# A gated transformer block in fp32 parts: the feed-forward stage rebuilt as one chunk pipeline, with its first weights split during the projection

## The reference

```python
xn = layernorm(x)                                   # x: (4, 1024, 256) float32
qkv = xn @ w_qkv                                    # 16 heads of 16
s = softmax(causal(q k^T / 4)) v @ w_out
f = xn
for i in range(6):                                  # feed-forward chain
    h = gelu(f @ W1[i].T + B1[i])                   # 256 -> 1024
    f = h @ W2[i].T + B2[i] + f                     # 1024 -> 256
    if i < 5: f = layernorm(f) * LN_G[i] + LN_B[i]
out = x + s * silu(f)
```

## Time and profile before

| | us |
|---|---|
| three executions | 1802.08, 1802.11, 1807.77 |
| median | 1802.11 |
| span of the profiled execution | 1806.1 |
| TensorE matmul busy | 1716.2 (95%) |
| VectorE busy | 1149.1 (64%) |
| ScalarE busy | 958.0 (53%) |
| GpSimd busy | 323.2 (18%) |

### The profile page before, as it was taken

The page is one execution under the profiler, slowest core; times in us unless marked ns, Lnnn a source line. Parts: engine busy times, 40 slices in busy tenths (PEclk is TensorE's granted clock), DMA queues, the critical chain, the costliest instruction groups (busy, mean ns, idle before and its releaser), DMA issues. The chain is left out here.

```text
span 1806.1 us, 33624 instructions
## 1 busy us (share of the span) xinstructions
PE 1716.2 (95%) x11664; PEld 1312.9 (73%) x11664; DVE 1149.1 (64%) x2325; ACT 958.0 (53%) x1364; POOL 323.2 (18%) x317
## 2 busy tenths in 40 slices
PE   6979999999999999999999999997999989999947
PEld 5869999999999989999999998875444433444236
DVE  7846666666666656666666643366877866877326
ACT  5834555555555545555555554432666665666723
POOL 3511111111111111111111111110121211121214
PEclk9989999999999999999999999998999998999969
DMA  6940000000000000000000050003474754574113
GB/s 206 306 140 13 12 17 16 13 12 17 13 9 12 17 16 12 13 17 12 16 12 12 0 83 24 23 24 64 76 112 75 109 84 73 88 107 73 48 57 137
DMA packets 104427, 97.97 MB, mean 54 GB/s; under 512 B 26636, under 2 KB 88588, under 8 KB 104316
## 3 DMA queue, kind: packets, MB, share of 16 engines
q1 hardware_dynamic: 104256, 96.39, 23.9%
q10 hardware_dynamic: 60, 0.10, 0.0%
HBM read 62.15 MB, written 29.62 MB: 51 GB/s over the span
## 5 line engine op out<-in xcount | busy, mean ns | idle before, releaser
L626 ACT ACTIVATE m_hid<-m_h_ps,m_b1s 128x512 f32<-128x512 f32 x384 | 264.3, 688 | 571.0 <-PE m_h_ps L752 558.9
L687 DVE TENSOR_TENSOR m_hidl<-m_hid,m_hidh 128x512 fp32r<-128x512 f32 x384 | 307.4, 809 | 323.9 <-ACT m_hidh L628 322.8
L129 DVE TENSOR_REDUCE mx<-a_s_ps 128x1 f32<-128x512 f32 (+3 forms) x570 | 341.2, 656 | 91.3 <-PE a_s_ps L117 87.8
L1003 ACT ACTIVATE a_prob<-a_st_ps 128x1024 f32<-128x1024 f32 (+1 forms) x320 | 289.9, 938 | 168.5 <-PE a_st_ps L1153 123.0
L752 PE MATMUL m_h_ps<-xth,shared 128*128 (+1 forms) x768 | 269.8, 397 | 12.3 <-DVE shared L655 12.2
L763 PE MATMUL m_y_ps<-shared,m_hidh 128*128 128x256 f32 x1536 | 277.9, 281 | 0.0
L628 ACT ACTIVATE m_hidh<-m_h_ps,m_b1s 128x512 fp32r<-128x512 f32 x384 | 261.8, 682 | 0.0
L763 PEld LDWEIGHTS m_y_ps<-shared,m_hidh 128*128 128x128 f32 x1536 | 246.6, 189 | 12.0 <-DVE m_hidl L687 0.4
L602 POOL TENSOR_TENSOR y<-y,m_b2s 128x1024 f32<-128x1024 f32 x47 | 112.8, 2400 | 708.3 <-DVE y L663 708.3
L763 PE MATMUL m_y_ps<-m_w2h,m_hidh 128*128 128x256 f32 x768 | 217.9, 284 | 0.6 <-DVE m_hidl L687 0.3
L763 PE MATMUL m_y_ps<-shared,m_hidl 128*128 128x256 f32 x768 | 215.8, 281 | 0.0
(11 more groups left out here) (115 smaller groups left out, 2648.3 us busy)
## 6 DMA issues: line engine op xcount, KB each, us to landing
q_parts<-p_part SPq DMA_DIRECT2D x16, 384.0 KB, 3.5
k_parts<-p_part SPq DMA_DIRECT2D x16, 384.0 KB, 3.0
m_raw<-w1t SPq DMA_DIRECT2D x48, 128.0 KB, 2.2
m_raw<-w2t SPq DMA_DIRECT2D x48, 128.0 KB, 2.4
shared<-q_parts SPq DMA_DIRECT2D x48, 128.0 KB, 4.6
shared<-k_parts SPq DMA_DIRECT2D x48, 128.0 KB, 7.7
a_qs<-q_parts SPq DMA_DIRECT2D x48, 128.0 KB, 4.6
a_ks<-k_parts SPq DMA_DIRECT2D x48, 128.0 KB, 7.4
```

What stands on the lines that cost most here:

```text
L129: return nc.vector.reduce_max(mx[:, half, first:first + heads, qt], scores, AX_X)
L626: nc.scalar.activation(hid[k % 2][:], h_ps[k % 2][:], ACT.Gelu, bias=b1s[s.par][:, k:k + 1])
L687: nc.vector.tensor_tensor(hidl[k % 4][:], hid[k % 2][:], hidh[k % 4][:].bitcast(F32), ALU.subtract).then_inc(low_done, 1)
L1003: nc.scalar.activation(prob[step % BUFS][:, j:j + heads, 0:hi - lo], unit_ps(unit), ACT.Exp).then_inc(exp_done, 1)
```

## The change: what it does

Projection: `norm` writes the rows straight into `xres`; `keep_high`, `keep_low` and `keep_rows` are gone. The loops are written out. After the four parts of group g, VectorE splits piece g of block 0's weights (`split_piece`). SyncE loads that piece (`weight_piece`), two ahead. x is loaded two groups ahead instead of three.

Feed-forward: `xth` and `xtl` are double buffers of one group. TensorE transposes the rows of slot t+1 in slot t, for every slot. The rows are updated in place in `xres`: VectorE adds y in two halves, GpSimd adds b2, VectorE takes statistics and applies mean and inverse deviation in one operation, GpSimd multiplies by LN_G and adds LN_B. `up` and `down` run as one sequence over 384 chunks. The score pieces have PSUM banks of their own and are spread over slots 42 to 47. The result stays in `xres`: `mlp_out`, its stores and its loads into `f_rows` are gone.

```diff
+def weight_piece(sp, keep, w1t, w2t, i, g, loaded):
+    w1v = w1t.rearrange("i (c p) h -> i p c h", p=P)
+    sp.dma_start(keep["raw1"][g % 2][:], w1v[i][:, :, P * g:P * (g + 1)]).then_inc(loaded[g % 2], 16)
+    sp.dma_start(keep["raw2"][g % 2][:], w2t[i, P * g:P * (g + 1), :]).then_inc(loaded[g % 2], 16)
+
+def split_piece(nc, dve, keep, par, g, high, high_count):
...
+    nc.vector.tensor_copy(w1h[:, :, cols], raw1[:])
+    nc.vector.tensor_copy(w2h[:, g, :], raw2[:]).then_inc(high, 1)
+    dve.wait_ge(high, high_count)
+    nc.vector.tensor_tensor(w1l[:, :, cols], raw1[:], w1h[:, :, cols].bitcast(F32), ALU.subtract)
+    return nc.vector.tensor_tensor(w2l[:, g, :], raw2[:], w2h[:, g, :].bitcast(F32), ALU.subtract)
...
 # project, SyncE
-                sp.dma_start(xtl[:, :, bass.ds(GT * g, GT)].bitcast(F32), gtl[u][:].bitcast(F32)).then_inc(gtl_stored[u], 16)
...
-                    if left > u:
-                        wait_apart(sp, normed, g + 4, sp_passed)
-                        load_x(g + 3, 1 - u)
-                    store(g, 0)
-                    if more:
-                        keep_low(g + 1, 1 - u)
-                    for m in range(1, 4):
-                        store(g, m)
...
+            for g in range(GROUPS):
+                if g + 2 < GROUPS:
+                    sp.wait_ge(normed, g + 1)
+                    load_x(g + 2)
+                    sp.wait_ge(piece_split, g + 1)
+                    weight_piece(sp, keep, w1t, w2t, 0, g + 2, piece_loaded)
+                for m in range(4):
+                    sp.wait_ge(part2_done, 4 * g + m + 1)
+                    rows = (qd if m < 2 else kd)[P * (m % 2):P * (m % 2) + P]
+                    sp.dma_start(rows[:, :, GT * g:GT * (g + 1)], part[m][:]).then_inc(part_stored[m], 16)
+                sp.wait_ge(v_copied, g + 1)
+                sp.dma_start(vd.rearrange("(g j p) d -> g p j d", p=P, j=TILES)[g], vout[g % 2][:]).then_inc(v_stored[g % 2], 16)
...
 # project, VectorE
+            for g in range(GROUPS):
+                if g + 1 < GROUPS:
+                    norm(g + 1)
+                split_rest(g, 0)
+                split_rest(g, 1)
+                if g + 2 < GROUPS:
+                    statistics(g + 2)
+                if g + 1 < GROUPS:
+                    low(g + 1)
+                split_rest(g, 2)
+                split_rest(g, 3)
+                dve.wait_ge(piece_loaded[g % 2], 32 * (g // 2 + 1))
+                split_piece(nc, dve, keep, 0, g, piece_high, g + 1).then_inc(piece_split, 1)
...
 # mlp, GpSimd
+                pool.wait_ge(y_added, 2 * (t + 1))
+                nc.gpsimd.tensor_tensor(xx, xx, b2s[i % 2][:].broadcast_to([P, TILES, DIM]), ALU.add).then_inc(b2_added, 1)
+                if t < NORMED:
+                    pool.wait_ge(var_ready, t + 1)
+                    nc.gpsimd.tensor_tensor(rstd[:], var[:], keep["mhalf"][:], ALU.pow).then_inc(rstd_ready, 1)
...
+                    pool.wait_ge(normed, t + 1)
+                    nc.gpsimd.tensor_tensor(xx, xx, lng[i % 2][:].broadcast_to([P, TILES, DIM]), ALU.mult).then_inc(scaled, 1)
+                    pool.wait_ge(scaled, t + 1)
+                    nc.gpsimd.tensor_tensor(xx, xx, lnb[i % 2][:].broadcast_to([P, TILES, DIM]), ALU.add).then_inc(x_ready, 1)
...
 # mlp, TensorE
+            turn(0)
+            for n in range(CHUNKS + 2):
+                if n < CHUNKS:
+                    up(n)
+                if n % CH == 2 and n // CH + 1 < SLOTS:
+                    turn(n // CH + 1)
+                for p in AT.get(n, ()):
+                    piece(p)
+                if n >= 2:
+                    down(n - 2)
```

More of the change, by code:

```diff
@@ L310, in _ @@
+            norm(0)
             dve.wait_ge(w_loaded, 16)
             nc.vector.tensor_copy(wh[:], w_raw[:]).then_inc(w_high, 1)
-            low(0, 0, 1)
+            low(0)
             dve.wait_ge(w_high, 1)
             nc.vector.tensor_tensor(wl[:], w_raw[:], wh[:].bitcast(F32), ALU.subtract).then_inc(w_split, 1)
-            statistics(1, 1, 1)
[L317 to L322, removed]
-                    split_rest(g, 0)
-                    split_rest(g, 1)
-                    if not last:
-                        statistics(g + 2, u, p + 2)
-                    if more:
-                        low(g + 1, 1 - u, p + 1 + u)
-                    split_rest(g, 2)
-                    split_rest(g, 3)
@@ L332, in _ @@
-            pairs(dve, body)
+            statistics(1)
+            for g in range(GROUPS):
+                if g + 1 < GROUPS:
[10 more added lines that the diff above has]
+                split_piece(nc, dve, keep, 0, g, piece_high, g + 1).then_inc(piece_split, 1)
@@ L408, in transpose @@
                 i.then_inc(transposed, 1)
[L410 removed]
+            transpose(0)
             pe.wait_ge(w_split, 1)
[L413 to L437 removed]
@@ L566, in slot @@
-            def slot(s):
-                if s.more:
-                    piece = GROUPS * (s.i + 1) + s.g
-                    sp.wait_ge(w_split, piece - 1)
-                    load_raw(s.i + 1, s.g, s.u)
-                    if s.second or (s.kind == "middle" and s.first and s.u == 1):
-                        if s.kind == "middle":
-                            sp.wait_ge(b2_added, GROUPS * s.i)
-                        load_bias(s.i + 1, 1 - s.par)
-                if s.kind == "last" and s.first and s.u == 1:
-                    sp.wait_ge(w2_done, CH * GROUPS * (BLOCKS - 1) + 4)
-                    for hg in range(2):
-                        load_stacks(sp, scratch, *stacks[hg], 0, hg, stacks_loaded)
-                if s.final:
-                    store_f(b2_added, s.t, s.eg, (s.u + 1) % 2)
@@ L802, in _, with turn @@
-            sweep(pe, slot, begin)
+            def turn(t):
+                if t >= GROUPS:
+                    pe.wait_ge(x_ready, t - GROUPS + 1)
+                if t:
+                    pe.wait_ge(xtl_done, t)
+                g = t % GROUPS
+                for c in range(HALVES):
+                    for j in range(TILES):
+                        i = nc.tensor.transpose(tr_ps[:, c, j * P:(j + 1) * P], xres[:, TILES * g + j, c * P:(c + 1) * P], ident[:])
+                i.then_inc(transposed, 1)
```

671 lines of the change are left out of this document (257 added, 414 removed).

## The result

The changed kernel takes 1827.9 us (median of 4 runs, 1825.61 to 1831.4); the kernel before, run beside it on the same chip, 1802.1 us (1800.42 to 1807.77). The ratio is 1.0143 with a 95% interval from 1.0123 to 1.0163: slower by 25.8 us. Forecast were 1831 and a range of 1813 to 1851.

The account below looks back on a forecast made before the run. TensorE was taken to bound the feed-forward stage; in the projection all engines were close to their limit. Terms 36.8 + 2 + 0 - 8.1 - 1.9 = +28.8 gave span 1834.9, median 1831 us, range 1813 to 1851.

Parts of the forecast that it names:

- Projection, +46.7 for +38.8: Projection: a cycle through SyncE's queue makes a group 17.1 us instead of 9.95, +36.8; TensorE's lower clock adds +2.
- my upper bound of 11.1: Projection: latest landing of x after a split's end, from 2.88 MB at 330 GB/s, 8.7 us; 10.3 was taken.
- S + 3.6: Projection: S is a split's end; x issued 3.6 us later, behind two weight transfers, four stores and v.
- Clock, +2: Projection: TensorE idles in spells of over 5 us and its clock drops, +2 us (ends 0 and +21).
- The rival of a clock that stays low: Projection: TensorE's clock stays at the low level, +21 instead of +2, 1850 us; chance 0.12.
- Feed-forward, -19.1 for -8.1: Feed-forward stage: chunks, 47 transpositions, restart and score pieces sum to 1125.0 us, -8.1 (ends -3 and -10).
- The restart: Start of feed-forward: TensorE restarts at the half clock, costing 2 us.
- End, -2.6 for -1.9: Feed-forward's end to attention's first matmul: a store falls away, b2 goes to GpSimd, -1.9 (ends -1 and -2.5).
- the mild cycle: Projection: next group's transfers overlap better, period 11 to 14 us, sum +0 to +15, 1802 to 1817; chance 0.06.
- a queue that catches up: Projection: stores are not late and it runs at TensorE's 9.2 us per group, time 1787; chance 0.05.
- waited for both of GpSimd's operations: Feed-forward: VectorE's subtraction blocked by GpSimd's LN_G and LN_B operations, 1.4 us per slot, about 1887; chance 0.04.
- The deciding point: Projection: it may cost 4.6 us more at most, a period of 10.6, for the kernel to be 0.3% faster.

Follow-up runs that it names:

- the first experiment: Changed kernel with the wait for the split and the next weight piece's load moved behind the store of the values in the projection's queue: 1808.2 us, ratio 1.0029.
- the second: Kernel of the first experiment with x loaded three groups ahead of its store rather than two: 1784.9 us, ratio 0.9905.
- the third experiment: Changed kernel with x three groups ahead and block 0's weights loaded and split in the feed-forward's first slot, not the projection: 1780.2 us, ratio 0.9882.

## Why the prediction was right, and where its terms were off

**Projection, +46.7 for +38.8 (36.8 and 2 for the clock).** The mechanism was right as written: the queue behind the split, x behind the stores, statistics, parts, next split. The splits end at 29.83, 49.33, 67.75, 86.63, 105.01 and 124.81, against 30.0 predicted for the first and 115.5 for the last. Five cycles are 95.0, or 19.0 each for 17.1. By its parts:

- From the split's end to the statistics on x: 11.6 in the mean (11.0 to 12.4) for 10.3, over my upper bound of 11.1. That bound was worked out from the bytes, and it was nearly the value: from 70 to 76 us the transfers are at a share of 1.02 and 335 GB/s (last row of the windows above), at which the 2.88 MB of a burst take 8.6 us. Taking less than the bytes say was the slip. The issues behind a split are also dearer than the half us each that I took from single ones in the earlier trace rows: two stores in a row took 1.22 and 2.27, where one of before took 0.56 (line below), and x was issued at S + 5.7 and not S + 3.6. It landed 5.8 later, for 5.0 in the earlier trace rows. Whether the full transfers make the issues longer, no run shows.

```profile
34.16 0.56 SPq L196 DMA_DIRECT2D q_parts<-p_part  x1
```

- From the statistics to the split's start: 4.27 for 4.9.
- The split: 3.1 for 1.9. Its two subtractions stretch to 1.27 and 1.38 since GpSimd's two parts, 2.58 together, run from 64.88; alone the last took 0.42. I had seen the surcharge in the earlier trace rows and then taken the lower value because the split begins first. It does, but only its two casts: the subtractions come when GpSimd is already at work.

From the end of the last cyclic split to the start of the last v matmul it took 16.9, to its end 17.0; predicted 16.4.

What decides is which engine begins first, instruction by instruction. In the cycle both casts begin before GpSimd (64.65 and 64.85, GpSimd at 64.88) and keep their 0.28. In the last group GpSimd begins first, and there the casts are stretched; the subtractions begin when its parts are done, at 141.53 + 2.32 = 143.85, and are not:

```profile
141.53 2.32 POOL L247 TENSOR_TENSOR p_part<-p_rest,p_part 128x512 bf16<-128x512 f32 x2 [0.33 <-ACT p_part L328]
141.57 1.26 DVE L144 CAST shared<-raw 128x256 fp32r<-128x256 f32 x1
142.75 1.24 DVE L145 CAST shared<-raw 128x256 fp32r<-128x256 f32 x1
144.03 0.42 DVE L147 TENSOR_TENSOR shared<-raw,shared 128x256 fp32r<-128x256 f32 x1
```

SBUF — State Buffer, § Who interferes with whom, of the Trainium skill says that a VectorE operation with two SBUF inputs contends with a GpSimd operation that reads SBUF, that a cast can contend too, where it runs in a 2-port mode, and that the order of issue decides which of the two waits. The trace agrees, with 1.27 and 1.38 for the subtractions of the cycle and 1.26 and 1.24 for the casts of the last group; in which mode the casts ran it does not show. Laid on the four instructions one by one, it puts the split's end one subtraction behind GpSimd's second part: 0.23 + 2.58 + 0.3 = 3.1, an estimate made with hindsight from 64.65, 64.88 and 67.75.

**Clock, +2.** The granted clock falls to its lower level, 1.2 GHz, in each idle spell's wake for 6.8 or 10.2 us (0.52 from 77.6 to 87.8). TensorE isn't on the cycle then, since it waits for `p_gtl` anyway, and the five cycles add up without it: no part of them is left for the +2. The rival of a clock that stays low did not come.

**Feed-forward, -19.1 for -8.1.** By my own sum: 384 chunks at 2.760 are 1059.8 us for 1075.2, the term that was mis-sized, because I carried the 2.80 over. 47 transpositions cost 0.87 each (a chunk with one takes 3.627), 40.7, for 37.6; each slot's first `down` also waits for the sums of the slot before. The restart took 1.8 for 2. The score pieces took 11.7 for 10.2. In the stage of before, the hole at slot 24 and the slow slot behind it had cost 4.5 us more than two plain slots, not 2.5. No trace of before shows a chunk faster than 2.80 away from the score pieces, and no experiment found what makes it so.

**End, -2.6 for -1.9.** In line.

**The rivals.** None of the four came: the period of 19.0 is beyond the mild cycle's 14 and far from a queue that catches up, and no subtraction took more than 2.65 us, so none waited for both of GpSimd's operations. The deciding point was off. I put it at a period of 10.6, because I counted only 10 us to be gained elsewhere. With 22 us to be gained it lies higher: at 15.8 the first experiment stands 0.3% above the kernel before, and at 10.63 the second stands 0.95% below. That the forecast came out near its centre is luck: two terms erred in opposite directions, by +7.9 and -11.0 us. The last stage gave another -3.8, which is within its scatter; the other differences are under 1 us.

That the rebuilt feed-forward stage is a gain by itself is shown by the third experiment: with the projection free of splits and x three ahead, the kernel is 21 us faster than before by the medians. By the two traces it is 28.7 (spans 1777.4 and 1806.1), and 16.4 of that are the stage's (103.1 to 1219.8, where the earlier trace rows give 1133.1). Against the trace with the loops written out, whose stage takes 1128.2, it is 11.5. The first two experiments show that the loss of the whole change is the order of one queue: moving a wait and a load in it turns +1.4% into -0.95%.

## What to carry to other kernels

A wait put into an in-order DMA queue costs what is queued behind it, and the cost multiplies where a load behind it feeds the very work that is waited for; follow that cycle once round, and its length is the new period. Put loads that feed the next step ahead of any wait for the present one, and load as many steps ahead as there are buffers. When VectorE and GpSimd meet, price each VectorE instruction by itself, by its operands and by which engine has begun first, not the group of them.

## What the runs showed that I had not expected

- The same twelve matmuls of 256 columns take 0.118 us a step in one program and 0.113 in another, at the granted clock 1.00 in both, independent of what the other engines do. TensorE: Matmul & The Clock Gate, § Back-to-back issue gap, of the Trainium skill gives N / 2.4 + 2.5 ns for an isolated gap, by which 256 columns are about 109 ns; for a sustained stream it has figures for 128 and 512 columns alone. Here the step was 4 to 9 ns above the former.
- Issues late in a burst take longer: 1.11 us for v and 1.17 for x as seventh and eighth behind the split, where they took 0.43 and 0.38 in the kernel before. In the first experiment, where x comes right behind four others, it took 0.51 and the weight piece ahead of it 1.24. What makes an issue long is not shown.
- With GpSimd's two more operations beside VectorE the mean subtraction took 1.14 us instead of 0.79, without any effect on a TensorE-bound slot.
